# Seven pairs in place of six in layer 1, with half of the weight sums made in PSUM in layer 0

## What is computed

```python
def cond(x, weights, condition):          # x: (32, 64, 1024)
    return jnp.einsum('bct,bcd->bdt', x, weights[condition])
# layer 0
x = x + (cond(x, L0_cond_weights, itok) @ ternary_project(L0_ffn_w) + L0_ffn_b)
# layer 1
w = (NF4_LEVELS[q_weight].reshape(-1, 64) * q_scale[:, None]).reshape(1024, 1024)
y = cond(x, L1_cond_weights, itok)
x = x + (einsum('bsi,oi->bso', y, w) + bias + 4.0 * (y @ lora_A.T) @ lora_B.T)
```

## Time and profile before

| | us |
|---|---|
| median of 3 runs | 361.86 (360.42 to 362.22) |
| the profiled execution | 361.14 |
| its span, first to last instruction | 359.3 |

### The profile page before, as it was taken

The page is one execution under the profiler, slowest core; times in us unless marked ns, Lnnn a source line. Parts: engine busy times, 40 slices in busy tenths (PEclk is TensorE's granted clock), DMA queues, the critical chain, the costliest instruction groups (busy, mean ns, idle before and its releaser), DMA issues.

```text
span 359.3 us, 5496 instructions
## 1 busy us (share of the span) xinstructions
PE 352.3 (98%) x1832; PEld 300.4 (84%) x1832; DVE 241.4 (67%) x362; ACT 161.9 (45%) x286; POOL 224.7 (63%) x146
## 2 busy tenths in 40 slices
PE   6999999999999999999999999999999999999996
PEld 5988788888888888888888888888888888888884
DVE  3879969896996899873799879355262452634523
ACT  2877467786886877752232314213041130321300
POOL 0658999986976888876520220866366663666632
PEclk9899999999999999999999999999999999999999
DMA  7995410854355245333221330304215032150202
GB/s 229 312 294 153 151 31 30 324 185 147 118 181 178 93 151 187 145 120 120 96 88 62 123 117 4 119 1 155 88 63 181 1 139 104 60 182 2 117 31 88
DMA packets 27838, 44.63 MB, mean 124 GB/s; under 512 B 8834, under 2 KB 17026, under 8 KB 27810
## 3 DMA queue, kind: packets, MB, share of 16 engines
q1 hardware_dynamic: 26322, 43.69, 35.2%
q10 hardware_dynamic: 1488, 0.59, 0.7%
HBM read 27.49 MB, written 16.78 MB: 123 GB/s over the span
## 4 chain that ended last, share of the span: by engine, by line
PE 92%; DVE 3%; issue 2%; DMA 1%; ACT 1%; SPq 0%; DVEq 0%; ACTq 0%
PE acc L1155 32%; PE acc L1193 32%; PE xT L1119 12%; PE acc L1135 8%; PE spare L1119 3%; PE acc L1220 2%; PE acc L1119 1%; DMA mix<-in_L_cond_weights 1%; PE acc L1222 1%; DVE hl L870 1%; DVE W L923 1%; PE xT L1202 0%; DVE side_p L914 0%; DVE side_n L911 0%; ACT spare L721 0%
## 5 line engine op out<-in xcount | busy, mean ns | idle before, releaser
L567 POOL TENSOR_TENSOR X<-X,bias 128x1024 f32<-128x1024 f32 x28 | 67.6, 2415 | 29.3 <-PE xT L1119 29.1
L1155 PE MATMUL acc<-T,hh 128*128 128x512 f32 x192 | 76.0, 396 | 0.0
L1155 PE MATMUL acc<-T,hl 128*128 128x512 f32 x192 | 75.0, 391 | 0.0
L721 ACT ACTIVATE spare<-q_raw 128x512 f32<-128x512 int32 x96 | 56.0, 598 | 19.2 <-DVE side_p L911 5.2
L1193 PE MATMUL acc<-W,hh 128*128 128x512 f32 x192 | 61.1, 389 | 0.0
L1019 DVE TENSOR_TENSOR X<-X,acc 128x512 f32<-128x512 f32 x36 | 24.8, 688 | 34.8 <-PE acc L1193 18.6
L1119 PEld LDWEIGHTS xT<-mix,X 128*128 128x128 f32 x352 | 42.7, 192 | 1.5
L1119 PE MATMUL xT<-mix,X 128*128 128x128 f32 x352 | 42.8, 275 | 0.0
L1155 PEld LDWEIGHTS acc<-T,hl 128*128 128x128 f32 x192 | 36.1, 188 | 7.4
L1193 PEld LDWEIGHTS acc<-W,hh 128*128 128x128 f32 x192 | 36.0, 188 | 7.5
L626 POOL TENSOR_TENSOR X<-X,ys 128x512 f32<-128x512 f32 x18 | 22.6, 1286 | 31.1 <-DVE ys L1008 31.1
(11 more groups left out here) (98 smaller groups left out, 650.5 us busy)
## 6 DMA issues: line engine op xcount, KB each, us to landing
out<-X SPq DMA_DIRECT2D x26, 512.0 KB, 2.7
X<-out SPq DMA_DIRECT2D x16, 512.0 KB, 3.4
X<-in_x SPq DMA_DIRECT2D x12, 512.0 KB, 3.4
q_raw<-in_L_ffn_q_weight SPq DMA_DIRECT2D x16, 256.0 KB, 2.9
w_in<-in_L_ffn_w SPq DMA_DIRECT2D x14, 256.0 KB, 5.8
x_first<-in_x SPq DMA_DIRECT2D x4, 512.0 KB, 5.5
out<-x_first SPq DMA_DIRECT2D x4, 512.0 KB, 6.8
out<-X SPq DMA_DIRECT2D x4, 256.0 KB, 2.0
```

Source lines behind the costliest of these rows:

```text
L567: pool.tensor_tensor(x_of(g), x_of(g), (bias1 if g >= NT else bias)[:, :], ALU.add).then_inc(s_xb, 1)
L721: act.activation(dst, q_raw[:, d % QS, :, :].rearrange("p o i -> p (o i)"), ACT.Copy, scale=slope, bias=offset).then_inc(s_line, 1)
L1155: mm = pe.matmul(acc[:, bank_of(q), :], a[:, k, :], b, start=(k == 0 and j == 0), stop=(k == KB - 1 and j == len(terms) - 1))
```

## The change

SB becomes NT + 2: two single tiles and seven pairs. So the weight sums have two single tiles in place of four. Two of the four are moved to layer 0:

- `keep_block(d)` (ScalarE): pieces of B11 and B12 are also copied whole from wT to SBUF, into the place of T2 or T3, viewed as plain float32.
- `sum_T13(d)` (VectorE): with piece B12 or B22 in wT, and after low_w(d), the kept block is subtracted in place in PSUM; wT then holds T1 or T3. `high_T13` (ScalarE) and `low_T13` (VectorE) copy its two parts to SBUF. turn_w of the next piece waits for low_T13 besides low_w.
- `sum_T24(u)` (VectorE) makes T2 and T4 in layer 1: five steps and one low part for each j, 24 in all, dealt over the four half tiles by SUMS_BY. `high_T24` is ScalarE's side.
- `lines_by(m)`: ScalarE draws at least the lines that VectorE's maxima before half tile m need.
- W01 and W23 hold (block, j%2) in another order, so that the four entries over the place of x_first are written from piece 4 on; the wait for its four stores moves to high_w(4).

```diff
-    SB = NT + 4
+    SB = NT + 2
...
-    NTS = 12
-    COMPLETE = ((T1, 3), (T3, 5), (T2, 6), (T4, 10))
+    NTS = 6
+    SUMS_BY = (0, 8, 15, 21, NTS * HB + 1)
...
+    def lines_by(m):
+
+        done = share(2 * NC * ND, m)
+        if done == 0:
+            return 0
+        d, c = divmod(done - 1, 2 * NC)
+        sign, j = divmod(c, NC)
+        return max(share(2 * NL * ND, m), 2 * NL * d + NL * sign + j + 2)
...
+            def keep_block(d):
+
+                j, r = divmod(d, 4)
+                act.wait_ge(s_wT, d + 1)
+                act.activation(as_is((T2, T3)[r], j), wT_flat, ACT.Copy).then_inc(s_asis, 1)
+
+            def high_T13(d):
+
+                j, r = divmod(d, 4)
+                act.wait_ge(s_T13, 2 * j + r)
+                act.activation(w1(0, (T1, T3)[r - 1], j), wT_flat, ACT.Copy).then_inc(s_T13h, 1)
...
                 for m in (NH * g, NH * g + 1):
                     for d in range(ND):
                         if turned_in(d) == m - 1:
+                            if d % 4 < 2:
+                                keep_block(d)
                             high_w(d)
                     if F <= g < SB - 1 and m % NH == 0:
                         high_x(g + 1, 0)
                         high_x(g + 1, 1)
                     elif m == NH * SB - 2:
                         left_A(0)
+                    for d in range(ND):
+                        if turned_in(d) == m - 1 and d % 4 in (1, 2):
+                            high_T13(d)
                     if g < NT:
-                        lines(share(per, m), share(per, m + 1))
+                        lines(lines_by(m), lines_by(m + 1))
...
+            def sum_T13(d):
+
+                j, r = divmod(d, 4)
+                dve.wait_ge(s_asis, 2 * (j + 1))
+                dve.tensor_tensor(wT_flat, wT_flat, as_is((T2, T3)[r - 1], j), ALU.subtract
+                                  ).then_inc(s_T13, 1)
+
+            def low_T13(d):
+                j, r = divmod(d, 4)
+                c = (T1, T3)[r - 1]
+                dve.wait_ge(s_T13h, 2 * j + r)
+                dve.tensor_tensor(w1(1, c, j), wT_flat, w1(0, c, j).bitcast(F32), ALU.subtract
+                                  ).then_inc(s_T13l, 1)
...
+                elif step == 0:
+                    dve.wait_ge(s_T13l, 2 * (j + 1))
+                    dve.tensor_tensor(as_is(T2, j), as_is(T2, j), w1(0, T3, j).bitcast(F32), ALU.add
+                                      ).then_inc(s_T2, 1)
...
                 pe.wait_ge(s_wn, d + 1)
                 pe.wait_ge(s_ys, NH * F)
                 need(pe, s_Wl, d)
+                if d % 4 in (2, 3):
+                    pe.wait_ge(s_T13l, 2 * (d // 4) + d % 4 - 1)
```

## The result

| | before | changed |
|---|---|---|
| median of 20 runs each, us | 361.11 (360.42 to 362.22) | 361.97 (361.28 to 363.02) |
| ratio | | 1.0023, 95% interval 1.0014 to 1.0032 |
| the profiled execution, us | 361.14 | 362.48 |
| its span, us | 359.3 | 360.6 |

What follows compares the result with a forecast made beforehand. TensorE, busy 352.3 of 359.3 us, was taken as the bound. Pairs -2.72 plus layer 0 losses 3.2 gave +0.5 us: 361.6 from the profiled 361.14, stated as 362.3 on the median 361.86; range 360.2 to 365.0.

Steps and rivals of the forecast that it cites:

- The pairs, -2.72 us: Layer 1: two tiles move from single to paired, saving TensorE 2.72 us, the same as 12 matmuls.
- The losses at the four turnings: Layer 0, pieces 1, 5, 9, 13: TensorE waits before the next turning; net of the old wait 3.2 us.
- The formula: Layer 0: TensorE's loss is low_w's start after the last turning's end, plus 2.65 plus 0.15 minus 3.51 us.
- G: Layer 0: the end of TensorE's last turning; without a wait the next starts 3.51 us later.
- d = 13: Layer 0, turning after piece 13: low_w 1.8 us after the last turning's end, a loss of 1.15 us.
- the idle time beside high_T13: Layer 0, VectorE at d%4 = 1: idle 0.76 us while ScalarE copies the high part, since nothing stands between.
- the 0.16 for d%4 = 2: Layer 0, VectorE: 0.16 us idle during the high part, as two low_x (1.20) stand there.
- Layer 1: nothing: Layer 1: the 24 sum steps over two single tiles cost TensorE nothing, with 3.7 us to spare.
- Only the smallest losses: Rival, layer 0: VectorE gets ahead, ScalarE's chain alone sets the four losses; net -1.5, 360.4 us; chance 0.17.
- VectorE the bound with its line waits kept: Rival, layer 0, groups d = 4 to 13: half the line waits stay; net +3.9, 365.8 us; chance 0.25.
- Late sums: Rival, layer 1: third product waits for its left side's sum after five GpSimd meetings; 2.0 us lost, 364.3; chance 0.06.
- the 3.7 us of cover: Layer 1, third product: VectorE's sums may come 3.7 us later before TensorE waits.

## Why the prediction held, step by step

I said 362.3 us; it is 361.97, and the change +0.8 us where the sum had +0.5. That the first two lie so close is partly luck. I put the sum on a median of 3 runs, 361.86; that of 20 runs is 361.11. On this base the sum gives 361.6, and the measured time is 0.4 above it. The mechanism, four waits at the named places against a full gain in the pairs, is the one that the trace shows.

- **The pairs, -2.72 us.** Exact in the trace (22.64 us a pair, no wait at a product); alone 2.8 us by the medians. Nothing of it went elsewhere.
- **The losses at the four turnings.** 1.53, 0.44, 0.6 and 1.15 us predicted; 1.56, 0.44, 0.69 and 1.37 measured. With the old wait taken off, 3.56 in place of 3.2. The formula, loss = (low_w start - G) - 0.71, gives 69.40 - 67.12 - 0.71 = 1.57 at piece 1, and the start of low_w(1), forecast for 68.96 on the start of before, came at 69.40 with a start 0.4 later. At piece 5 the loss is set by ScalarE's chain, as forecast (low_w 1.15 us after G).
- **The term that was too small is that of d = 13.** low_w(13) stood 161.89 - 159.80 = 2.09 us after G, and I had 1.8 (and 1.8 - 0.71 is 1.1, not 1.15). I let VectorE take 28.51 - 0.7 + 3.3 = 31.1 us from low_w(9) to low_w(13); it took 161.89 - 130.52 = 31.4. The 0.7 us of small waits of before did vanish. Two others came, one for a line behind piece 9 and one at low_w(12) for ScalarE's high part:

```profile
134.00 0.69 DVE L956 SCALAR_TENSOR_TENSOR side_p<-side_p,spare 128x512 f32<-128x512 f32 x1 [0.24 <-ACT spare L748]
...
152.33 0.69 DVE L968 TENSOR_TENSOR W<-acc,W 128x512 fp32r<-128x512 f32 x1 [0.32 <-ACT W L758]
```

  Ahead of that high part ScalarE now copies the kept block of the same piece, which holds it from 151.23 to 151.71; I had counted keep_block at pieces 1, 5, 9 and 13 only. Against these 0.56 us the idle time beside high_T13 was 0.66 and not 0.76, and the 0.16 for d%4 = 2 did not show: 0.56 - 0.10 - 0.16 = 0.3 us, what was missing.

- **Layer 1: nothing.** The pairs were to begin at 201.7 and began at 202.50: 0.4 of the difference is the start, 0.36 the losses. The 24 sum steps fit; the left side's sum began at 199.90, ahead of the pairs.
- **The rivals.** *Only the smallest losses* needed VectorE to get ahead before each piece. It did at piece 5 alone. *VectorE the bound with its line waits kept* fell with the line waits; but its premise, that VectorE's work is above a group's time, was right (from low_w(5) to low_w(9) it took 30.69 us, where TensorE without waits needs 29.96) and is what the experiments kept meeting: putting maxima elsewhere gave nothing back, and releasing the bank early made it worse. *Late sums* did not come: the sums that met a bias addition (2.76 us at 179.22, 1.02 at 192.02) lay long before anyone needed them. The price of a meeting was wrong, though. I had 1.15 us from one row, and the trace of before has a sum that lost 2.1:

```profile
174.61 2.84 POOL L567 TENSOR_TENSOR X<-X,bias 128x1024 f32<-128x1024 f32 x1
...
175.24 2.76 DVE L936 TENSOR_TENSOR plain_sums<-plain_sums,W 128x512 f32<-128x512 f32 x1
```

Two more meetings of this size, not four, would have used up the 3.7 us of cover.

What I did not see is how cheaply the loss could be avoided. I treated the chain of sum, high part and low part as fixed, since it must run in the bank; only the sum must. The low parts of T have no reader before layer 1.

## What to carry to other kernels

When a step holds a resource that the bound engine waits for, keep in it only what needs that resource, and give the rest to an engine whose queue the bound engine does not wait for, even if it is twice as slow there (1.30 against 0.69 us). A saving on the bound engine is counted in durations; a cost put on its feeder is counted from when the feeder arrives, so read for each place how late it already is. If the feeder is full, moving its work to another stretch only moves the loss (1.0025 against 1.0023), while an order that takes a wait out of its queue does help: 0.8 us for the result between, 2.4 for the parts of the T sum behind lines and maxima.

## What was not expected of the hardware

VectorE's subtraction of two SBUF operands took up to 2.85 us (0.69 alone) when it met GpSimd's 128 x 1024 addition of 2.4 us, while VectorE's instructions with a PSUM operand kept their 0.68 us beside the same GpSimd work. Of the eight low parts in the version with the sum in SBUF, two began after GpSimd's addition had ended and took 0.69 us. Six began while it ran, and each of them ended 0.54 to 0.56 us after it, whenever it had begun. The last of them, the addition that it met, and GpSimd's next one:

```profile
172.32 0.81 DVE L983 TENSOR_TENSOR W<-W_sums,W 128x512 fp32r<-128x512 f32 x1
...
170.17 2.41 POOL L607 TENSOR_TENSOR X<-X,ys 128x1024 f32<-128x1024 f32 x1 [1.32 <-DVE ys L945]
...
172.54 2.84 POOL L594 TENSOR_TENSOR X<-X,bias 128x1024 f32<-128x1024 f32 x1
```

VectorE ended at 173.13, GpSimd's first addition at 172.58. So VectorE's instruction waits for the addition that runs, and the price of a meeting is what is left of that addition, up to 2.2 us here. The last row is the other way round: this addition began while VectorE's low part ran, and took 0.4 us longer than its 2.4. So the engine that comes second pays.
